# Edge sum of a graph kernel: block numbers loaded one word at a time, inside a step instead of ahead of it

## The chip, the cores and the metric

The kernel runs on one core of a Trainium2 chip. The metric is device time in microseconds, from one launch. Three runs of the kernel before gave 3587.72, 3590.77 and 3591.53 us; the median, 3590.77 us, is the time to compare with.

## What is computed

A graph has 12500 nodes with 64 features and 400000 edges, sorted by their target node `dst`. Three message-passing rounds run over the same edges: a mean over neighbours, then two convolutions that also add a projection of each edge's own 64 attributes. Since the projection is linear, the kernel needs the sum of the edge attributes at each target node only once; that sum is what the changed loop computes. Cut down to it:

```python
agg = segment_sum(x[src], dst);  deg = segment_sum(1, dst)
h = relu(concat(x, agg / max(deg, 1)) @ W_fc + b_fc) + x @ W_res + b_res
x1 = layernorm(x + h)
# each of the two convolutions:
msg = h[src] @ Wm + bm + edge_attr @ We + be     # segment_sum(edge_attr, dst) is shared by both
out = segment_sum(msg, dst) + h @ Ws + bs
# result: layernorm(x1 + conv2(relu(conv1(x1))))
```

## The kernel before

The 12500 nodes lie in 98 blocks of 128. The program has a preparation, then round 0, then the **edge sum**, then rounds 1 and 2. Each engine has its own instruction stream, written out by hand; semaphores order them. Only the edge sum is touched by the change. It starts about 1537 us into the profiled execution and ends at about 2021 us.

The 400000 edges are 625 groups of 5 x 128. The edge sum goes through `ESTEPS` = 728 steps; a step takes one group and the block of 128 target nodes to which it adds (a group that spans two blocks takes two steps). Which group and block a step has depends on the data, so both lists are made at the start of the program and kept on partition 0: group numbers as words in `path`, block numbers as bytes in `steps`, four to a 32-bit word. All buffers are rings of `EB` = 8, so step n uses slot h = n % 8. In one step:

- SyncE loads the group's edge attributes into `feats[h]` (L1540).
- GpSimd (POOL) makes `rel_e[h]`, the target's lane within the block for every edge (L1291), after VectorE has used the slot (`e_mark`).
- VectorE (DVE) compares `rel_e[h]` with the lane numbers and gets 0/1 marks, 128 x 640 in f16 (L921, the **comparison**). It waits for `e_hot` (ScalarE has read that slot's last marks; on even h, L919) and `e_rel` (L920).
- ScalarE (ACT) copies the marks of two steps to f32 (L1416), after `e_mark`, and signals `e_hot`.
- TensorE (PE) multiplies attributes by marks into PSUM bank h, 10 matmuls (L1179), and signals `e_mm[h]`.
- VectorE adds the PSUM bank of the step `LAG` = 6 before into the sum of its block, 128 x 128 in f32 (L932, the **addition**). It waits for `e_mm` (L929) and for its own last addition, `e_add` (L930), since two additions may go to the same block. The block is known only at run time: register operations, recorded at L932, cut the byte out of a loaded word and turn it into an address.

So VectorE's stream is comparison, addition, comparison, addition, with register operations between. The loop body is written out for `TURNS` = 7 rounds of the ring, 56 steps; the loop over it (L913) runs 13 times. The bytes come into registers by `load_blocks(frm, n)`: one load instruction (TENSOR_LOAD, at L466) that fetches n/4 words into n/4 registers of VectorE's sequencer. The returned list has four expressions for each word (a mask, or a shift and a mask); the trace shows them at L932, where they are used. Other places call it too: the sum of gathered rows in all rounds loads 8 bytes, two words, at a time. A similar helper `load` (L458) fetches words of `path`; VectorE calls it for one word at the end of each round.

Of the kernel before, what the change touches and what calls it, by code (L numbers as in the profile page):

```python
# [105 lines left out]
def gnn_program(nc, step_c, first_row, x, src, dst, edge_attr, W_fc, b_fc, W_res, b_res,  # L106
# [8 lines left out]
    D0, D1 = B0 * P, END * P  # L115
    REG, (RUNS, CSTEPS) = regions(), runs()
    BACK = max(k for _, _, _, k, _ in RUNS)
    CG = -(-CSTEPS // P)
    HIS = BLOCKS
# [13 lines left out]
    EB = 8  # L133
# [3 lines left out]
    TURNS = 7  # L137
# [10 lines left out]
    CH = 512 // VC  # L148
    CW = CG * P
    spans_of = [(s0, (REG + [(0, 0, 0, 0, CW)])[n + 1][4], wd) for n, (_, _, wd, _, s0) in enumerate(REG)]  # L150
    PIECES = 16
    HB, RING = 4, 16
# [13 lines left out]
    assert TP > WHOLE and WHOLE % 16 == 0 and BLOCKS <= P  # L166
    assert UNION >= YW >= BLOCKS * D and G * F1 <= 512 and 0 < GI <= ITERS and all(b <= 2 * GI or b - n >= 2 * GI for n, b in ((r[1], r[0] + r[1]) for r in REG)) and B0 >= 0 and DB % 2 == 0 and WPB % HB == 0
    assert all(n % 2 == 0 and s0 % P == 0 and sum(d) * WD // wd % RING == 0 for _, n, wd, ds, s0 in REG for d in ds) and HIS % 2 == 0 and (SETS - SETS % 2) * G >= T + BLOCKS - 1

    ctx = ExitStack()  # L170
    with ctx:
# [127 lines left out]
        sums_e = af[:, :].rearrange("p (b c) -> p b c", c=P)  # L299
# [163 lines left out]
        def load_blocks(frm, n):  # L463

            words = steps[0:1, :].bitcast(I32)
            _, packed = nc.values_load_multi_w_load_instructions(  # L466
                words[0:1, bass.ds(frm, n // 4)], engines=(ENG.DVE,), min_val=0,
                max_val=(BLOCKS - 1) * 0x01010101,
                skip_runtime_bounds_check_because="four block numbers, each clamped when the path was made")
            return [nc.s_assert_within(b, 0, BLOCKS - 1, skip_runtime_bounds_check_because="one of the four block numbers")  # L470
                    for v in packed for b in (v & 0x7F, (v >> 8) & 0x7F, (v >> 16) & 0x7F, v >> 24)]

        def flat(v):
            return v.rearrange("p b d -> p (b d)")
# [3 lines left out]
        def _(dve):  # L478
# [58 lines left out]
            for b in range(-(-CG // CH)):  # L537
                cols = slice(b * CH, min(b * CH + CH, CG))
                n = cols.stop - cols.start
# [90 lines left out]
            for b in range(3):  # L630
                cols = slice(b * GP, min(b * GP + GP, SG))
                n = cols.stop - cols.start
# [66 lines left out]
            for c0, c1, landed in ((0, SG // 2, s_g[0]), (SG // 2, SG, s_last)):  # L699
                dve.wait_ge(landed, 16 * (c1 - c0))  # L700
                n, cols = c1 - c0, slice(c0 * P, c1 * P)
# [25 lines left out]
            for r in range(3):  # L727
# [82 lines left out]
                if r == 0:  # L810
# [5 lines left out]
                    for b0, blocks, wd, deeps, s0 in REG:  # L816
                        upto, pair = steps_upto(wd, deeps)
                        many = at_once(wd)
                        with dve.Fori(0, blocks // 2) as i:
                            for j in range(2):  # L820
# [3 lines left out]
                                for q in range(upto[j][0], upto[j][WPB]):  # L824
                                    n, s = q % RING, bass.ds(i * pair + (q + s0), many)
# [11 lines left out]
                                    if part == 0:  # L837
                                        dve.wait_ge(b_used[j], it + (1 + j))
                                        if b0 < 2 * GI:
                                            bs = load_blocks((it * 2 + j) * (GW // 4), GW)  # L840
# [4 lines left out]
                                    elif part == 1:  # L845
                                        dve.wait_ge(b_red[j], it + 2)
                                        to = flat(acc_all[:, bass.ds(i * 2 + (b0 + B0 + j), 1), :])
                                        V.tensor_tensor(to, to, part_d[:, j, :], ALU.add).then_inc(s_add[0], 1)
                                    else:
                                        k = part - 2  # L850
                                        dve.wait_ge(s_add[0], before + (k + 1))
                                        if k < G:
                                            to = flat(acc[:, bass.ds(bs[k], 1), :])
# [7 lines left out]
                    for j in range(2):  # L861
# [4 lines left out]
                        to = acc[:, END - 2 + j, :]  # L866
# [5 lines left out]
                if r:  # L872
                    for first, end in ((0, GI), (GI, ITERS))[0:1 + (GI < ITERS)]:
                        with dve.Fori(0, end - first) as i:
                            for j in range(2):
# [8 lines left out]
                                to = feat[:, bass.ds(i * 2 + (first * 2 + B0 + j), 1), :]  # L884
# [27 lines left out]
                first_block = SETS * GW + GW + EDGE0 - LAG  # L912
                with dve.Fori(0, ESTEPS // EB, TURNS) as turn:  # L913
                    for n in range(EB * TURNS):
                        i, h = turn + n // EB, n % EB
                        if n % (2 * EB) == 0:
                            bs = load_blocks(turn * (EB // 4) + (first_block + n) // 4, min(2 * EB, EB * TURNS - n))
                        if h % 2 == 0:
                            dve.wait_ge(e_hot[h // 2], i + 1)  # L919
                        dve.wait_ge(e_rel[h], i + 1)  # L920
                        marks = V.tensor_tensor(mark_e[:, h, :, :].rearrange("p j (c u) -> p j c u", u=2),  # L921
                                                lane16[:, 0:P].rearrange("p (c u) -> p c u", u=2).unsqueeze(1)
                                                .to_broadcast([P, EG, P // 2, 2]),
                                                rel_e[:, h, :, :].unsqueeze(2).to_broadcast([P, EG, P // 2, 2]),
                                                ALU.is_equal)
                        if h % 2:
                            marks.then_inc(e_mark[h // 2], 1)
                        b = (h - LAG) % EB
                        dve.wait_ge(e_mm[b], i + (2 if h >= LAG else 1))  # L929
                        dve.wait_ge(e_add, i * EB + (h + EB))  # L930
                        to = flat(sums_e[:, bass.ds(bs[n % (2 * EB)], 1), :])
                        V.tensor_tensor(to, to, ps[:, b, 0:P], ALU.add).then_inc(e_add, 1)  # L932
                last = load_blocks((SETS * GW + ESTEPS + GW + EDGE0 - LAG) // 4, EB)
                for k in range(LAG):
                    dve.wait_ge(e_mm[EB - LAG + k], ESTEPS // EB + 1)
                    dve.wait_ge(e_add, ESTEPS + k + EB)
                    to = flat(sums_e[:, bass.ds(last[k], 1), :])
# [650 lines left out]
```

## Time and profile before

| | before |
|---|---|
| median of three runs | 3590.77 us |
| profiled execution: span | 3585.2 us |
| edge sum: stretch of the span | 1537 to 2021 us, 484 us |
| busy in that stretch: PE / DVE / ACT / POOL | 441.9 / 441.8 / 431.9 / 207.7 us |
| VectorE's comparison / addition, mean of one | 484 / 280 ns |
| loads at L466 in that stretch | 52: shortest 520 ns, median 965, longest 985 |
| mean transfer rate in that stretch | 246 GB/s |

The span runs from the first to the last instruction of the profiled execution. The single runs are 2.5 to 6.3 us above it; what the profile adds or leaves out at the ends is not in the table. PE, DVE, ACT, POOL and SP are TensorE, VectorE, ScalarE, GpSimd and SyncE. A "q" behind an engine's name marks an instruction that its sequencer runs itself (register arithmetic, loads into registers, branches): these are not counted as busy, and the engine proper may work meanwhile. A comparison and an addition in a row overlap by about 0.08 us at each seam, so busy time of a group can add up to more than the time that passes.

### The profile page before, as it was taken

What the parts mean: (1) busy time and instruction counts of PE and PEld (TensorE: products, weight loads), DVE (VectorE), ACT (ScalarE), POOL (GpSimd) and SP (SyncE); (2) the same over time, 40 slices, a digit from 0 to 9 for tenths busy, and PEclk for the clock granted to TensorE, in tenths of its full rate; (3) what the DMA queues carried; (4) which work ended last, traced back from release to release, by engine and by line L of the source; (5) the groups of instructions that cost most, each with busy time, mean ns of one, the idle gap of its engine ahead of it and who ended that gap; (6) DMA issues with size and microseconds to landing.
All of it is one profiled execution on the core that took longest, in us unless ns stands there. A gap on an engine that the chain in (4) does not pass through costs nothing.

```text
span 3585.2 us, 114923 instructions
## 1 busy us (share of the span) xinstructions
PE 3167.6 (88%) x39408; PEld 2958.1 (83%) x39408; DVE 2339.3 (65%) x5369; ACT 1613.7 (45%) x2096; POOL 2021.8 (56%) x2292
## 2 busy tenths in 40 slices
PE   0239999999999999889999889999999889999995
PEld 0127988888888888778888879999999889999995
DVE  8779998888888888779999682333333423333335
ACT  0123677878999999788988650000000400000000
POOL 6761234445666666534444256666666666666664
PEclk9869999999999999999999979999999999999998
DMA  3521455556666666668888429999999599999996
GB/s 92 134 18 70 167 194 198 218 213 233 238 240 251 251 238 240 245 207 247 248 246 247 147 93 400 403 402 402 402 402 403 202 354 403 402 402 402 402 402 241
DMA packets 232872, 959.10 MB, mean 268 GB/s; under 512 B 44815, under 2 KB 144285, under 8 KB 173818
## 3 DMA queue, kind: packets, MB, share of 16 engines
q1 hardware_dynamic: 186027, 884.48, 65.0%
q0 software_dynamic: 46784, 73.84, 6.8%
q8 instruction: 33, 0.54, 0.1%
q14 instruction: 28, 0.23, 0.0%
HBM read 694.75 MB, written 263.40 MB: 267 GB/s over the span
## 4 chain that ended last, share of the span: by engine, by line
PE 68%; DVE 11%; issue 8%; POOL 6%; DVEq 3%; ACT 2%; DMA 2%; SPq 0%; ACTq 0%; POOLq 0%
PE ps L1109 48%; PE ps L1132 10%; DVE union L805 5%; PE ps L1179 4%; PE ps L1101 3%; POOL abuf L1213 3%; DVE union L921 2%; ACT union L1416 1%; DVE abuf L932 1%; POOL union L1213 1%; PE ps L1069 1%; DVEq L466 1%; DVEq L932 1%; PE ps L1188 1%; POOL abuf L1255 0%
## 5 line engine op out<-in xcount | busy, mean ns | idle before, releaser
L1271 POOL DMA_INDIRECT msg<-y_tab,idx x1368 | 1531.1, 1119 | 1041.9 <-ACT idx L1377 652.0
L1109 PE MATMUL ps<-union,abuf 128*128 128x192 bf16 x14896 | 1265.3, 247 | 13.9 <-DVEq L782 10.2
L1109 PEld LDWEIGHTS ps<-union,abuf 128*128 128x128 f16 x14896 | 1226.7, 98 | 21.2 <-issue 10.6
L1398 ACT ACTIVATE abuf<-ps 128x784 f16<-128x784 f32 x1216 | 1000.7, 823 | 239.9 <-PE ps L1132 212.3
L805 DVE TENSOR_TENSOR union<-lane,union 128x1568 f16<-128x1568 f16 (+3 forms) x1440 | 949.5, 710 | 31.0 <-PE ps L1132 27.1
L1109 PE MATMUL ps<-early,abuf 128*128 128x195 bf16 x7546 | 853.4, 249 | 0.0
L1109 PEld LDWEIGHTS ps<-early,abuf 128*128 128x128 f16 x7546 | 677.1, 99 | 100.9
L1132 PE MATMUL ps<-union 128*128 128x392 f16 (+2 forms) x4288 | 689.5, 288 | 52.4 <-DVE union L805 47.1
L1377 ACT ACTIVATE idx<-src_g 128x6 int32 (+1 forms) x228 | 46.4, 205 | 1280.2 <-PE ps L1101 1277.9
L1179 PE MATMUL ps<-union 128*64 128x128 f32 x7280 | 444.4, 278 | 48.2 <-ACT union L1416 48.1
L1179 PEld LDWEIGHTS ps<-union 128*64 128x64 f32 x7280 | 394.1, 137 | 98.4 <-DVE abuf L932 79.2
L1416 ACT ACTIVATE union<-union 128x1280 f32<-128x1280 f16 x364 | 432.9, 1259 | 55.9 <-DVE union L921 53.9
L797 DVE TENSOR_TENSOR acc<-acc,ps 128x64 f32 (+1 forms) x918 | 203.7, 222 | 364.2 <-DVE acc L797 211.2
L1132 PEld LDWEIGHTS ps<-union 128*128 128x128 f16 x4288 | 362.9, 108 | 92.3 <-issue 48.3
L921 DVE TENSOR_TENSOR union<-lane,rel_e 128x640 f16<-128x640 f16 x728 | 352.5, 484 | 41.7 <-issue 40.3
L1291 POOL TENSOR_TENSOR rel_e<-early,base_e 128x10 f16 x728 | 208.4, 305 | 287.5 <-DVE union L921 271.1
L880 DVE TENSOR_REDUCE part_d<-ps 128x64 f32<-128x192 f32 x152 | 54.4, 358 | 459.2 <-PE ps L1109 459.2
L786 DVE TENSOR_TENSOR hot_g<-code_g,lane 128x768 f16<-128x768 f16 x228 | 218.0, 956 | 70.2 <-DVE acc L797 69.2
L932 DVE TENSOR_TENSOR abuf<-abuf,ps 128x128 f32 x728 | 203.5, 280 | 1.8 <-PE ps L1179 1.1
L1101 PE MATMUL ps<-msg,hot_g 128*128 128x64 bf16 (+1 forms) x4104 | 167.2, 194 | 5.5 <-DMA msg<-y_tab,idx 5.5
L1101 PEld LDWEIGHTS ps<-msg,hot_g 128*128 128x128 f16 x4104 | 157.0, 98 | 6.0 <-DMA msg<-y_tab,idx 6.0
L854 DVE TENSOR_TENSOR acc<-acc,ps 128x65 f32 x456 | 99.5, 218 | 56.8 <-DVE acc L854 37.9
(229 smaller groups left out, 1241.4 us busy)
## 6 DMA issues: line engine op xcount, KB each, us to landing
abuf<-a_dram SPq DMA_DIRECT2D x304, 1568.0 KB
a_dram<-abuf SPq DMA_DIRECT2D x76, 3136.0 KB
union<-in_edge_attr_dram SPq DMA_DIRECT2D x728, 160.0 KB, 2.9
msg<-y_tab,idx POOLq DMA_INDIRECT x1368
y_tab<-union SPq DMA_DIRECT2D x28, 336.0 KB, 2.2
abuf<-in_x_dram SPq DMA_DIRECT2D x28, 224.0 KB, 3.4
y_tab<-early SPq DMA_DIRECT2D x7, 682.5 KB, 5.5
out_dram<-union SPq DMA_DIRECT2D x2, 800.0 KB, 3.5
```

The lines of the kernel that those rows point to most:

```text
L786: V.tensor_tensor(hot_g[:, j * G:(j + 1) * G, :], code_g[:, bass.ds((it * 2 + j) * G, G)].unsqueeze(2).to_broadcast([P, G, P]), lane16[:, ...
L805: return V.tensor_tensor(to.rearrange("p s (c u) -> p s c u", u=2), lanes.unsqueeze(1).to_broadcast([P, n, width // 2, 2]), codes[:, which ...
L921: marks = V.tensor_tensor(mark_e[:, h, :, :].rearrange("p j (c u) -> p j c u", u=2), lane16[:, 0:P].rearrange("p (c u) -> p c u", u=2).uns ...
L932: V.tensor_tensor(to, to, ps[:, b, 0:P], ALU.add).then_inc(e_add, 1)
L1101: last = nc.tensor.matmul(tile_ps(r, j, k), hot_g[:, s, :], msg[:, s, c * width_of[r]:(c + 1) * width_of[r]], start=c == 0, stop=c == 2)
L1109: last = nc.tensor.matmul(ps[:, bank, 0:3 * width_of[r]], abuf[:, buffer, hi * P:(hi + 1) * P], ycols[r][:, hi, :], start=hi == 0, stop=hi ...
L1132: nc.tensor.matmul(ps[:, w % 4, 0:WIN].rearrange("p (h d) -> p h d", d=WD)[:, :, d0:d0 + wd], hot_c[:, n, WIN:WIN + P], hot_c[:, n, 0:HIS ...
L1179: last = nc.tensor.matmul(ps[half:half + D, h, 0:P], feats[:, h, j * D:(j + 1) * D], hot_e[:, h, j, :], start=j < 2, stop=j >= EG - 2)
L1271: pool.indirect_dma_start(msg[:, s, 0:3 * width_of[r]], None, y_tab[r], bass.IndirectOffsetOnAxis(ap=idx[:, s:s + 1], axis=0)).then_inc(ga ...
L1291: nc.gpsimd.tensor_tensor(rel_e[:, h, :, :], flat(dst_e[:, bass.ds(grp[h], 1), :]).unsqueeze(2) .to_broadcast([P, EG, 2]), base_e[:, bass. ...
L1398: A.activation(abuf[:, j, :].rearrange("p (h w d) -> p w h d", w=WPB, d=WD) [:, w:w + 2, :, :], ps[:, w % 4:w % 4 + 2, 0:WIN].rearrange("p ...
L1416: A.activation(hot_e[:, h:h + 2, :, :], mark_e[:, h:h + 2, :, :], ACT.Copy)\
```

## The change

Before, VectorE loads block numbers ahead of the comparison of every sixteenth step of the body: at n = 0, 16 and 32 four words, at n = 48 the two words that are left. Afterwards it loads one word at every fourth step, and the load stands between the comparison and the addition of that step. In the 56 steps of a body that is 14 loads of one word in place of 4 loads with 14 words together; over the 13 passes, 182 loads in place of 52. The same bytes reach the same additions. Nothing else differs.

```diff
                 with dve.Fori(0, ESTEPS // EB, TURNS) as turn:
                     for n in range(EB * TURNS):
                         i, h = turn + n // EB, n % EB
-                        if n % (2 * EB) == 0:
-                            bs = load_blocks(turn * (EB // 4) + (first_block + n) // 4, min(2 * EB, EB * TURNS - n))
                         if h % 2 == 0:
                             dve.wait_ge(e_hot[h // 2], i + 1)
                         dve.wait_ge(e_rel[h], i + 1)
@@ -925,10 +923,12 @@
                                                 ALU.is_equal)
                         if h % 2:
                             marks.then_inc(e_mark[h // 2], 1)
+                        if n % 4 == 0:
+                            bs = load_blocks(turn * (EB // 4) + (first_block + n) // 4, 4)
                         b = (h - LAG) % EB
                         dve.wait_ge(e_mm[b], i + (2 if h >= LAG else 1))
                         dve.wait_ge(e_add, i * EB + (h + EB))
-                        to = flat(sums_e[:, bass.ds(bs[n % (2 * EB)], 1), :])
+                        to = flat(sums_e[:, bass.ds(bs[n % 4], 1), :])
                         V.tensor_tensor(to, to, ps[:, b, 0:P], ALU.add).then_inc(e_add, 1)
```

## Rows read from the trace of the kernel before

**Rows 1.** Edge sum, busy us: PE, PEld, DVE, ACT, POOL; PEclk, DMA share, GB/s.

```profile
1537.00:2021.00 484.00, 441.88 (x7240) 391.97 (x7240) 441.79 (x1456) 431.94 (x364) 207.73 (x725) 0.99 0.81 246
```

**Rows 2.** Waits in the edge sum: us in total, times, longest us.

```profile
ACT union L1416 <- DVE union L921: 53.9, 55, 4.8
...
DVE union L921 <- issue: 40.3, 51, 1.3
DVE union L921 <- POOL rel_e L1291: 1.4, 1, 1.4
DVE abuf L932 <- PE ps L1179: 1.1, 2, 0.6
```

**Rows 3.** VectorE in order of time, around a four-word load inside the body.

```profile
1882.96 0.28 DVE L932 TENSOR_TENSOR abuf<-abuf,ps 128x128 f32 x1
1884.03 0.49 DVE L921 TENSOR_TENSOR union<-lane,rel_e 128x640 f16<-128x640 f16 x1 [0.79 <-issue]
1884.43 0.28 DVE L932 TENSOR_TENSOR abuf<-abuf,ps 128x128 f32 x1
```

**Rows 4.** The chain, 1902.6 to 1906.9 us: start us, us, what.

```profile
1903.82 0.06 DVEq L466
1903.87 0.04 issue
1903.91 0.29 DVEq L466
...
1904.48 0.02 DVEq L920
...
1904.55 0.09 DVE union L921
...
1904.69 0.04 DVEq L932
1904.73 0.03 issue
1904.77 0.06 DVEq L932
...
1906.69 0.07 issue
1906.76 0.06 DVE abuf L932
```

**Rows 5.** VectorE in order of time, around the two-word load and the loop's end.

```profile
1903.92 0.28 DVE L932 TENSOR_TENSOR abuf<-abuf,ps 128x128 f32 x1
...
1904.95 0.28 DVE L932 TENSOR_TENSOR abuf<-abuf,ps 128x128 f32 x1
...
1909.15 0.28 DVE L932 TENSOR_TENSOR abuf<-abuf,ps 128x128 f32 x1
...
1911.09 0.28 DVE L932 TENSOR_TENSOR abuf<-abuf,ps 128x128 f32 x1
```

**Rows 6.** The chain across the loop's end, 1909 to 1911.8 us.

```profile
1909.53 0.97 DVEq L466
1910.50 0.03 issue
...
1910.68 0.09 DVE union L921
```

**Rows 7.** Loads at L466 in the edge sum: ns min/median/max.

```profile
L466 DVEq TENSOR_LOAD <-steps x52: 520/965/985, 1548.3 to 2020.6; - x52
```

**Rows 8.** VectorE's loads of one word at L458, whole span.

```profile
L458 DVEq TENSOR_LOAD <-path x3: 321/322/323, 1513.7 to 3553.0; - x3
```

**Rows 9.** A two-word load in round 0, then VectorE's work in that window.

```profile
L466 DVEq TENSOR_LOAD <-steps x1: 525/525/525, 844.4 to 844.4; - x1
...
843.82 1.64 DVE L805 TENSOR_TENSOR union<-lane,union 128x512 f16<-128x512 f16 x3
```

**Rows 10.** ScalarE's copies in the edge sum, in order of time.

```profile
1899.26 6.07 ACT L1416 ACTIVATE union<-union 128x1280 f32<-128x1280 f16 x5
```

## The prediction

> **What bounds the kernel now.** I read first how busy each engine is in the edge sum, since nothing else is touched. In its 484 us TensorE and VectorE are both busy for 442 us and ScalarE for 432 us [rows 1]. Three engines near 90% say only that none has much room, so the next view is who waits for whom. ScalarE idles 53.9 us in 55 waits, all for VectorE's comparison, and VectorE idles 40.3 us in 51 waits that the trace calls "issue": no semaphore is late, its own sequencer has not delivered the next instruction. VectorE waits 1.4 us for GpSimd and 1.1 us for TensorE in the whole stage [rows 2]. So VectorE sets the pace, the others follow, and the only idle time of VectorE is made in its sequencer. There were 52 loads in the stage [rows 7] and 51 such waits.
>
> The timeline gives the pace. From the addition at 1904.95 to that at 1909.15 there are 7 steps, 4.20 us, so 0.60 us a step without a load [rows 5]. 728 steps of 0.60 are 436.8 us. ScalarE's five copies in 6.07 us, the last of them about 1.26 us long, are 1.20 us for two steps [rows 10]: that is VectorE's pace handed on, and its 364 copies could run in 437 us at most.
>
> **What the old loads cost.** Addition to addition across a load, less 0.60:
> - four words inside the body: 1884.43 - 1882.96 = 1.47, an excess of 0.87 us [rows 3]; two in each pass (n = 16 and 32);
> - two words at n = 48: 1904.95 - 1903.92 = 1.03, an excess of 0.43 us [rows 5];
> - four words at the loop's end, with the branch: 1911.09 - 1909.15 = 1.94, an excess of 1.34 us [rows 5].
>
> One pass: 2 x 0.87 + 0.43 + 1.34 = 3.51 us. Thirteen passes: 45.6 us. Check: 436.8 + 45.6 = 482.4 of 484 us [rows 1]. This is the whole amount that the change can move; it vanishes and is replaced by what the new loads cost.
>
> **What one new load takes.** The trace has four words at 0.965 us (median) and two at 0.52 [rows 7, 9], and three loads of one word on the same engine at 0.321 to 0.323 us [rows 8]. The line through the longer ones (0.22 us a word) gives 0.30. I take 0.32, the measured one. Those three ran while VectorE was idle, the new ones run under a comparison. The nearest row for that: in round 0 a two-word load that began at 844.4 and took 0.525 lies wholly inside three f16 comparisons in a row that kept VectorE busy from 843.82 to 845.46 [rows 9]; it took no longer than others, nor did the sequencer wait for the engine to drain. So bounds are 0.30 below and 0.525 (a two-word load) above, and the value lies near the lower one.
>
> The Trainium skill, "DMA: Bandwidth & Descriptors", section "Latency and other measured facts", speaks against this change: it gives a floor of about 600 ns for a `tensor_load` and says that the compiler unrolls it four times to amortize that. By it, the 182 new loads would cost 0.28 us more each than I reckon, an estimate of +51 us on the sum below, and the kernel would end near 3630 us. The trace disagrees already: a two-word load takes 0.52 us and a one-word load 0.32 [rows 7, 8].
>
> **How much of it is covered.** Before, the load ended and only then could the comparison be sent. Now the comparison is sent first and the load runs beside it; but the addition's address needs the word, so all that follows the load in the sequencer stands in front of the addition. Step by step, for a body load:
> - The sequencer ends its wait for `e_rel` (L920) 0.07 us before the previous addition starts (1906.69 against 1906.76) [rows 4].
> - From that wait's end to the first register operation of L932, without a load between, 0.19 us (1904.50 to 1904.69): the comparison is sent and the value for L930 is made [rows 4].
> - Into this comes an address operation of 0.06 us and 0.04 behind it [rows 4], the load of 0.32 [rows 8], and 0.03 behind the load [rows 6]: 0.45 us.
> - L932's register operations: 1904.69 to 1904.83, 0.14 us; and 0.05 from a sequencer's instruction to the start on an idle engine (L920's end 1904.50, comparison 1904.55) [rows 4].
>
> That is 0.83 us from L920, so 0.76 from the previous addition, against 0.60. With the rows' rounding 0.14 to 0.17; I take 0.15 us. The comparison covers the other 0.3 us of every load. The wait for the addition before (`e_add`) is over by then and costs nothing more. There are 13 such loads in a pass.
>
> At the loop's end the old load of 0.97 and 0.03 behind it go, so the comparison starts at 1910.68 - 1.00 = 1909.68 [rows 6]. Then 0.14 to L932's operations, 0.35 for the load (no address operation stood at this place), 0.14 and 0.05: the addition at 1910.36, 1.21 after the one at 1909.15, an excess of 0.61 us.
>
> One pass: 13 x 0.15 + 0.61 = 2.56 us; thirteen passes: 33.3 us. Saved: 45.6 - 33.3 = 12.3 us. The profiled execution would have a span of 3585.2 - 12.3 = 3572.9 us, and the median, 5.6 us above its span, becomes 3590.8 - 12.3 = **3578.5 us**, 0.34% less. The lever is long: 10 ns on each of 182 loads are 1.8 us.
>
> **What is queued behind the load.** On VectorE the waits for `e_mm` and `e_add`, the addition, and then the next comparison. A late addition keeps only VectorE waiting: TensorE may overwrite a bank after an addition made two steps earlier, which always comes before the comparison that TensorE needs anyway. The late next comparison reaches ScalarE, TensorE and GpSimd, as the old stalls did, now in portions of 0.15 and 0.61 instead of 0.43 to 1.34 us. With the stage at about 471 us, ScalarE (437) and TensorE (442 busy) stay under it. DMA share is 0.81 of its engines at 246 GB/s [rows 1] and would be asked for 3% more. Rounds 1 and 2 start earlier and stay as they are.
>
> **Rivals.**
> - *The one-word load costs what a two-word load costs, 0.525 us* (slower). It would be a price of each load rather than of each word, or a load stretched under an f16 comparison. 0.205 x 182 = 37.3 us more: 3616 us. From 0.39 us a load on (12.3 / 182 = 0.07 above 0.32) the kernel is slower. Against it are rows 8 and 9. Chance 0.12.
> - *More register work in front of the addition* than before: another address operation per load, or one that used to lie in the comparison's shade. One of 0.10 us (0.06 and its gap [rows 4]) on every load: +18.2, 3597 us; on half of them no change in the time. The trace cannot show how the new address is made. Chance 0.15.
> - *More cover*: the sequencer runs ahead of the engine. If it reaches the load some 0.10 us sooner than by L920's row, the excess is 0.05: 13 x 13 x 0.10 = 16.9 us less, 3562 us. For it: the engine finishes the addition before the comparison starts, while the sequencer has sent both. Against: the order of L920, comparison, L930 in the chain leaves it no such lead. Chance 0.12.
> - *The gain goes elsewhere*: stalls spread evenly leave ScalarE or GpSimd no pause to catch up, and VectorE begins to wait for `e_rel` or `e_mm`. In stretches of 16 steps at 0.60 us it waited for neither [rows 2], and the new mean step of 0.65 is slower than that. Time near 3590. Chance 0.06.
>
> **How the numbers follow.** The forecast has a chance of 0.50; its own range is 3572 to 3585 us (load of 0.29 to 0.36 us). Another 0.05 is for what I do not see. A measurement of this kernel can tell about 0.2%, 7.2 us, from no change. Faster than 3583.6: most of the forecast (0.46), the case of more cover (0.12) and a little of the rest (0.02), 0.60. Within: 0.20, from the forecast's edge, half or more of the register case and the last rival. Slower than 3598: 0.20, from the dear load, the rest of the register case and the unseen. For 8 in 10 the range must take in most of the cover case and most of the register case but not the dear load: 3563 to 3600 us.
>
> **What would show it.** In the profile after: 182 loads at L466's successor in the stage, of 0.30 to 0.33 us; VectorE's "issue" waits moved from the comparison to the addition at n % 4 = 0; additions 0.75 us apart there and 0.60 elsewhere; at the loop's end 1.21 instead of 1.94; the stage 471 to 472 us. ScalarE's waits for the comparison fall from 53.9 to about 42 us. The prediction is wrong if loads are longer than 0.39 us, if more than one register operation stands around each load, or if VectorE's waits name GpSimd or TensorE.

## The result

The changed kernel is slower: 3654.68 us (median of five runs, 3644.68 to 3668.36) against 3588.83 (five runs, 3585.16 to 3591.53). The ratio is 1.0185, with a 95% interval of 1.0162 to 1.0208. I had forecast 3578.5 us, 0.34% faster, with a range of 3563 to 3600.

In the three later sets of runs the kernel before fell into two groups, near 3588 and near 3608 us (14 of 25, 10 of 23 and 10 of 32 runs in the upper one), and so did some variants; the groups are treated below, and the length of the edge sum does not depend on them.

The waits of the changed kernel in the edge sum, total us, times, longest; they answer to [rows 2]:

```profile
engine line waited for: us in total, times, longest us
...
ACT union L1416 <- DVE union L919: 94.2, 134, 5.2
...
DVE union L919 <- issue: 45.2, 12, 4.6
DVE abuf L932 <- issue: 15.2, 60, 0.3
...
DVE abuf L932 <- PE ps L1179: 11.6, 26, 0.6
```

VectorE's "issue" waits ahead of the comparison (L919 now) were 51 of 40.3 us together. There are 12 left, and they last 45.2 us: one for each return of the loop, up to 4.6 us. The waits of the addition are new. The 60 "issue" waits of 15.2 us look like those that I had foreseen at the loads, but they are not: by their place in the pass, 13 stand at its first step and 39 at the short pauses at steps 14, 34 and 54 that are described below, and only 8 elsewhere; at a load in the body the engine idles only 0.03 to 0.06 us, 0.10 at most. And there are 26 waits for TensorE, 11.6 us against 1.1. The loads themselves are not to blame, as the source view of L466 in the stage shows (ns min/median/max):

```profile
L466 DVEq TENSOR_LOAD <-steps x183: 299/305/541, 1537.1 to 2078.1; - x183
```

Around one load in the body, in order of time, and the chain there, which answers to [rows 4]:

```profile
1904.40 0.28 DVE L932 TENSOR_TENSOR abuf<-abuf,ps 128x128 f32 x1
1904.60 0.48 DVE L919 TENSOR_TENSOR union<-lane,rel_e 128x640 f16<-128x640 f16 x1
1905.13 0.29 DVE L932 TENSOR_TENSOR abuf<-abuf,ps 128x128 f32 x1
```

```profile
1904.50 0.30 DVEq L466
...
1904.95 0.04 DVEq L932
1905.00 0.03 issue
1905.03 0.06 DVEq L932
1905.09 0.05 issue
1905.13 0.12 DVE abuf L932
```

Addition to addition is 0.73 us: an excess of 0.13. So far the forecast holds. Then the loop's end, which answers to [rows 6]:

```profile
1909.70 0.04 DVEq L913
1909.74 0.03 issue
1909.77 0.06 DVEq L913
1909.83 0.25 DVE abuf L932
1910.08 4.42 issue
1914.50 0.05 DVEq L913
...
1914.67 0.10 DVE union L919
```

The closing branch runs at 1909.77, and the next instruction of the loop (L913) starts at 1914.50. Between them VectorE's sequencer does nothing and waits for nothing that has a semaphore. This return is the longest of the twelve: from the start of the branch to that of the next instruction they take 3.4 to 4.7 us, 3.9 in the mean. In the kernel before, the same two instructions lay 0.3 us apart, and the load followed:

```profile
1909.12 0.06 DVEq L913
1909.18 0.25 DVE abuf L932
1909.43 0.06 DVEq L913
1909.49 0.04 issue
1909.53 0.97 DVEq L466
```

A pause of this kind in each pass is new, and the page of the profile says what happens in it. The queue lists, before and after (packets, MB, share of 16 engines):

```profile
q14 instruction: 28, 0.23, 0.0%
```

```profile
q14 instruction: 88, 0.72, 0.1%
```

60 more packets of instructions, five for each of the 12 returns of the loop, of 8192 bytes each; if the short pauses described below, 128 instructions apart, lie at their bounds, that is 64 bytes an instruction. VectorE's loop is fetched anew in every pass, as the later runs bear out. The program has 115183 profiled instructions against 114923: 260 more, 20 for each of 13 passes (14 loads and 13 address operations where there were 4 and 3). The loop has 360 instructions instead of 340.

The pause has a sequel on TensorE. Busy us by stretch (PE, PEld, DVE, ACT, POOL, then the granted clock, DMA share and GB/s), for most of a pass, the pause, what follows it, and the pass after:

```profile
1880.00:1910.00 30.00, 29.26 (x470) 25.28 (x468) 28.63 (x92) 27.85 (x24) 13.63 (x44) 1.00 0.84 246
1910.00:1914.60 4.60, 2.52 (x41) 2.04 (x40) 0.08 (x1) 1.19 (x1) 0.36 (x2) 1.00 0.85 251
1914.60:1924.00 9.40, 6.29 (x62) 6.29 (x64) 7.12 (x22) 6.21 (x5) 2.85 (x10) 0.64 0.29 84
1924.00:1953.00 29.00, 28.25 (x457) 24.30 (x453) 27.73 (x89) 26.80 (x22) 13.63 (x44) 1.00 0.83 246
```

TensorE stood still for 5 us (to 1917.7), and for a good part of the next 9 us its granted clock was at the lower of its two levels, 1.2 instead of 2.4 GHz. The products of the first steps came late, and VectorE's additions waited for them:

```profile
1919.63 0.29 DVE L932 TENSOR_TENSOR abuf<-abuf,ps 128x128 f32 x1 [0.36 <-PE ps L1179]
...
1921.71 0.29 DVE L932 TENSOR_TENSOR abuf<-abuf,ps 128x128 f32 x1 [0.61 <-PE ps L1179]
```

The lower clock came back where it costs more. After the edge sum TensorE folds the sums (L1188), which took some 22 us at full clock before. Before, and then after (same columns):

```profile
2025.00:2045.00 20.00, 19.72 (x177) 19.72 (x177) 1.24 (x3) 5.97 (x10) 0.00 (x0) 1.00 0.00 1
```

```profile
2082.00:2102.00 20.00, 19.63 (x100) 19.64 (x100) 1.30 (x3) 3.45 (x6) 0.00 (x0) 0.55 0.00 1
2102.00:2122.00 20.00, 20.00 (x96) 20.00 (x95) 0.00 (x0) 3.12 (x6) 0.00 (x0) 0.50 0.00 0
```

196 folding products took 22.1 us before and 40.4 after. No pause of the loop stands right ahead of them: the clock was full from 2046.6 to 2084.2 us (PEclk is 1.00 from 2047 to 2082), and TensorE had idled 1.4 us between its last edge product and the first folding product. Whether the pauses have a part in this fall is not shown; the runs e5 and e11 below are about it. In sum, of the two profiled executions (3664.1 against 3585.2 us, 78.9 more): 57.1 in the edge sum, 20.4 between its last addition and round 1's first dense product (145.8 against 125.4), 1.4 in the rest. The profiled execution is one of the two slowest of the five. The two fastest, 3644.68 and 3650.21 us, lie 56 and 61 us above the median of before, which is about what the edge sum alone takes, and their mean clock is higher (0.959 against 0.954 and 0.955); so the 20 us of the folding probably belong to some of the runs only.

### The profile page after: what moved, and what is told of

It is laid out like the page before. It is cut to its first block, busy times and chain, and to the rows that moved or that the text cites. A ratio compares the mean times of both kernels' runs of the same rounds, so it can differ in the third digit from the quotient of the medians.

```text
span 3664.1 us, 115183 instructions
## 1 busy us (share of the span) xinstructions
PE 3222.9 (88%) x39408; PEld 3003.6 (82%) x39408; DVE 2358.7 (64%) x5369; ACT 1629.4 (44%) x2096; POOL 2030.2 (55%) x2292
## 4 chain that ended last, share of the span: by engine, by line
PE 65%; DVE 12%; issue 10%; POOL 6%; DVEq 4%; DMA 2%; ACT 1%; SPq 0%; POOLq 0%; ACTq 0%
PE ps L1109 47%; PE ps L1132 10%; DVE union L805 5%; PE ps L1101 3%; POOL abuf L1213 3%; DVE union L919 3%; DVE abuf L932 2%; PE ps L1179 2%; DVEq L466 1%; DVEq L932 1%; PE ps L1188 1%; POOL union L1213 1%; PE ps L1069 1%; DMA abuf<-in_x_dram 1%; ACT union L1416 0%
## 5 line engine op out<-in xcount | busy, mean ns | idle before, releaser
L1179 PE MATMUL ps<-union 128*64 128x128 f32 x7280 | 478.6, 286 | 70.9 <-ACT union L1416 61.2
L1179 PEld LDWEIGHTS ps<-union 128*64 128x64 f32 x7280 | 418.2, 143 | 131.3 <-DVE abuf L932 110.1
L1416 ACT ACTIVATE union<-union 128x1280 f32<-128x1280 f16 x364 | 448.6, 1268 | 97.3 <-DVE union L919 94.2
L1291 POOL TENSOR_TENSOR rel_e<-early,base_e 128x10 f16 x728 | 220.0, 321 | 332.9 <-DVE union L919 316.8
L919 DVE TENSOR_TENSOR union<-lane,rel_e 128x640 f16<-128x640 f16 x728 | 352.8, 485 | 46.6 <-issue 45.2
L932 DVE TENSOR_TENSOR abuf<-abuf,ps 128x128 f32 x728 | 206.2, 283 | 35.1 <-issue 15.2
```

The source lines that it names most:

```text
L1179: last = nc.tensor.matmul(ps[half:half + D, h, 0:P], feats[:, h, j * D:(j + 1) * D], hot_e[:, h, j, :], start=j < 2, stop=j >= EG - 2)
L1291: nc.gpsimd.tensor_tensor(rel_e[:, h, :, :], flat(dst_e[:, bass.ds(grp[h], 1), :]).unsqueeze(2) .to_broadcast([P, EG, 2]), base_e[:, bass. ...
L1416: A.activation(hot_e[:, h:h + 2, :, :], mark_e[:, h:h + 2, :, :], ACT.Copy)\
```

## The experiments

The columns of the table below are read from each profile: the mean time from one closing branch of the loop to the next; the edge sum from the first comparison to the last; and q14's packets. "Place" is where the loop's last instruction falls if VectorE's stream is counted in blocks of 128 from the block in which the loop begins: three blocks end at 384. It comes from the trace of the changed kernel. Beside the pause at the loop's end it shows three shorter ones of about 0.33 us in a pass, ahead of the 96th, the 224th and the 352nd instruction, 128 apart; the loop therefore begins at the 34th instruction of a block. (The addition of the last step is sent before the branch and starts after it; it is not counted to the next pass. When the expectations below were written I had counted it, and their places are one too low.) Kernel before: 33 + 340 = 373. After: 33 + 360 = 393, nine over.

| run | place of the loop's end | pass, us | edge sum, us | q14 | median, us (runs) |
|---|---|---|---|---|---|
| before | 373 | 37.15 | 483.6 | 28 | 3588.8 (5) |
| after | 393 | 41.89 | 540.7 | 88 | 3654.7 (5) |
| e1 after, shifted 104 | 369 | 36.02 | 469.5 | 29 | 3582.7 (10) |
| e2 before, shifted 19 | 392 | 44.07 | 567.1 | 88 | 3687.2 (4) |
| e3 before, shifted 104 | 349 | 37.20 | 483.9 | 29 | 3599.1 (10) |
| e4 two words, late | 379 | 36.59 | 476.6 | 28 | 3582.9 (10) |
| e5 after, shifted 97 | 362 | 35.97 | 469.4 | 30 | 3595.4 (12) |
| e6 before, shifted 12 | 385 | 44.32 | 569.3 | 89 | 3695.1 (2) |
| e7 before, shifted 13 | 386 | 44.33 | 569.6 | 88 | 3694.2 (2) |
| e8 before, 60 products | 373 | 37.13 | 483.4 | 28 | 3600.3 (12) |
| e9 one word, early, shifted 97 | 362 | 37.14 | 482.8 | 29 | 3607.7 (8) |
| e10 four words, late | 373 | 36.85 | 479.9 | 28 | 3585.8 (8) |
| e11 before, 8 products | 373 | 37.15 | 483.5 | 28 | 3588.2 (12) |
| e12 after, shifted 98, 8 products | 363 | 36.03 | 469.6 | 30 | 3573.6 (9) |

n increments moved the loop by n - 1 instructions: so many more instructions of VectorE stand ahead of it in the traces, and the short pauses of e2, e6 and e7 lie where they should by it (ahead of the 77th, the 84th and the 83rd instruction). The 98 inside a branch are taken as 98; no trace shows them, since they do not run. Each set of runs has its own runs of the kernel before, on the same chip: median 3605.0 of 25 beside e1 to e4, 3592.2 of 23 beside e5 to e8 (on another chip than e1 to e4 and e9 to e12), 3590.6 of 32 beside e9 to e12.

**Is it the code's position?** The loop is left alone and moved.

```diff
                 step(V.memset(sums_e[:, 0:HALF, :], 0.0))
+                for _ in range(105):              # e1 on the changed kernel, e3 on the one before; e2: 20
+                    dve.sem_inc(s_pad, 1)
                 dve.wait_ge(s_lde, 32)
```

> The changed kernel, with 105 idle semaphore increments on VectorE ahead of the edge sum, which move its loop 104 instructions further into VectorE's instruction stream. Theory A (code reloads: the loop of 360 instructions lies over four blocks of 128 instructions and is fetched again in every pass; moved, it lies within three): VectorE's queue of instruction fetches falls from 88 packets to about 30, the 4.3 us pause at each loop end falls to about 0.7, the stage is 470 us, and the time is 3575 to 3582 us (some us of the increments themselves included). Rival B (the loads themselves or their place are dear, whatever the code's position): no change, about 3655 us.

Measured: 3582.66 us, ratio to before 0.9953 (0.9932 to 0.9973). The page's line for the fetch queue:

```profile
q14 instruction: 29, 0.24, 0.0%
```

The pauses are gone, with every load still there. The edge sum is 14.1 us shorter than before. The time is at the upper end of the forecast plus 0.7 us, because the increments took 0.093 us each, 9.7 us together.

> The kernel before, untouched in its loop, with 20 idle increments ahead of it: the loop of 340 instructions moves 19 further and now ends 7 instructions inside a fourth block. Theory A: it gets the pauses of the changed kernel: about 58 us more in the edge sum and 20 us more behind it, since TensorE's clock is at its lower level there: 3650 to 3670 us. Rival B: 3589 to 3590 us, as before.

Measured: 3687.15 us, ratio 1.0228 (1.0177 to 1.0279). The old loop, untouched, gets the pauses, and they cost more than I expected: 83 us more in the edge sum, not 58. The chain at a return of its loop:

```profile
1928.07 4.22 issue
1932.29 0.09 DVEq L916
1932.38 0.04 issue
1932.41 0.96 DVEq L467
```

A pause of 4.22 us, and behind it still the four-word load of 0.96: the two add up. (Lines are shifted by the increments' three.)

> The kernel before with 105 idle increments, five times as many as in the run with 20; its loop lies within three blocks again. Theory A: 3589 to 3594 us, the increments' own time alone. If idle increments themselves cost time (rival C): more than the run with 20.

Measured: 3599.13 us, ratio 1.0007 (0.9982 to 1.0031); 7 of 10 runs lie at 3595.9 to 3600.8, some 10 us above the lower group of before, which is what 105 increments take. Rival C is out: more increments cost less than 20 did. These three runs show the cause: the loop's position in VectorE's stream, not what is in it.

**Is there an edge?** The increments stand further down from here on, where VectorE waits for the target rows.

```diff
+                for _ in range(13):               # e6 on the kernel before; e7: 14; e5, on the changed one: 98
+                    dve.sem_inc(s_pad, 1)
                 dve.wait_ge(s_pc, 1 + 2 * BC + BE)
```

> The kernel before with 13 idle increments. Its loop moves by 12 instructions, and by the positions read from the trace of the changed kernel its last instruction, the closing branch, is the last of the third block. Theory A, if a loop may fill three blocks to the last instruction: passes of 37.1 us, 28 or 29 fetches, 484 us for the edge sum. If the fetch looks ahead of the branch: already slow, passes of 41 us or more.

> One increment more than in the run with 13: the closing branch is the first instruction of a fourth block. Theory A: 88 fetches, a pause of about 4 us in every pass, passes of 41 to 42 us, an edge sum of 540 us and more. A cause that grows with the number of instructions (and has no edge) would show no difference between 13 and 14.

Measured: both slow and alike, 3695.13 and 3694.23 us, passes of 44.3 us, 89 and 88 fetches. For e6 I had written down a look ahead of the branch as the alternative, but the trace shows that the place was off by one instead. One of e6's short pauses stands in every pass right ahead of the closing branch, which is therefore the first instruction of the fourth block and not the last of the third. The chain at a return of e6 (L916 is the loop's line: first its register operation, then the branch):

```profile
1842.13 0.04 DVEq L916
1842.17 0.07 issue
1842.24 0.27 DVE abuf L935
1842.51 0.04 issue
1842.55 0.06 DVEq L916
1842.61 4.49 issue
1847.11 0.09 DVEq L916
```

and the same two instructions in e2, where the border lies elsewhere:

```profile
1927.69 0.04 DVEq L916
1927.73 0.03 issue
1927.76 0.06 DVEq L916
```

The branch starts 0.42 us after the register operation in e6 and 0.07 in e2. In e7 the pause stands one instruction earlier, ahead of the register operation. So both runs are past the border, no look ahead is needed to explain them, and no run has a loop that ends exactly at it. There is an edge: the old loop is fast where it ends at 373 and slow from 385 on, 12 instructions of shift cost as much as 13, and 104 cost nothing; with e4, fast at 379, the first slow place lies between 380 and 385.

**What are the loads worth without the pause?**

> The changed kernel with 98 idle increments, now placed where VectorE waits some 7 us for the target rows to be prepared, so that they cost 1 to 2 us instead of 9.7. Theory A (code position): the loop lies in three blocks, the edge sum is 14 to 15 us shorter than in the kernel before, and the time is 12 to 14 us under the lower of the two groups into which the runs of the kernel before fall (3587 us), so 3573 to 3576 us. Rival: the gain of the run with 105 increments came from something else that the increments did; then this one is not faster by what the increments no longer cost.

Measured: 3595.41 us, ratio 0.9989 (0.9969 to 1.0009). The edge sum is as expected, 469.4 us, 14.2 less than before. The time is not: 11 of 12 runs lie at 3590.9 to 3599.1, one at 3580.5. The profile has the reason, in the folding behind the edge sum:

```profile
2015.00:2035.00 20.00, 19.89 (x104) 19.89 (x104) 1.07 (x3) 3.58 (x6) 0.00 (x0) 0.57 0.01 1
2035.00:2055.00 20.00, 19.95 (x94) 19.76 (x93) 0.00 (x0) 3.59 (x7) 0.00 (x0) 0.50 0.00 0
```

The clock was at the lower level from 2017.6 on and the folding took 39.9 us, with no pause in the loop at all: the pauses are not needed for this fall. TensorE had idled 1.5 us ahead of the folding. What this kernel won in the edge sum, it lost to the clock. The increments also delayed the loop by 4 us, not by 1 to 2.

> The changed kernel with two words at every eighth step instead of one at every fourth, at the same place in the step. Its loop has 346 instructions and, unshifted, ends 6 short of the fourth block. Theory A: no pauses; a two-word load in front of the addition costs 0.34 us (0.13 measured for one word, and 0.21 for the second), so 6 x 0.34 + 0.92 = 3.0 us a pass against 3.5 before: 3581 to 3584 us. Rival B (place of the load): clearly slower than before, half the loads, so some 30 us more.

```diff
-                        if n % 4 == 0:
-                            bs = load_blocks(turn * (EB // 4) + (first_block + n) // 4, 4)
+                        if n % 8 == 0:
+                            bs = load_blocks(turn * (EB // 4) + (first_block + n) // 4, 8)
...
-                        to = flat(sums_e[:, bass.ds(bs[n % 4], 1), :])
+                        to = flat(sums_e[:, bass.ds(bs[n % 8], 1), :])
```

Measured: 3582.92 us, ratio 0.9976 (0.9949 to 1.0003), 7 of 10 runs at 3580.1 to 3584.9. The excess is 0.35 us for a body load and 0.82 at the loop's end, 2.9 us a pass (3.0 reckoned); the edge sum is 7.0 us shorter. No pause, and nothing is shifted: 346 instructions fit where 360 do not.

> One word at every fourth step, but ahead of the comparison as in the kernel before, with 98 covered increments so that the loop lies in three blocks. It differs from the covered shifted run of the changed kernel in the place of the load alone. Theory (the load's place is worth the difference between a stall of 0.22 us ahead of the comparison, by the old stalls' slope of 0.22 us a word, and 0.13 us behind it): 13 x 0.22 + 0.68 = 3.5 us a pass over 33.6, so passes of 37.1 us against 35.97, and an edge sum of 484 us against 469.4. If the place is worth nothing: 36.0 us a pass.

```diff
+                        if n % 4 == 0:
+                            bs = load_blocks(turn * (EB // 4) + (first_block + n) // 4, 4)
                         if h % 2 == 0:
                             dve.wait_ge(e_hot[h // 2], i + 1)
...
-                        if n % 4 == 0:
-                            bs = load_blocks(turn * (EB // 4) + (first_block + n) // 4, 4)
```

Measured: passes of 37.14 us and 0.22 us of excess for a body load, as expected; 3607.69 us, ratio 1.0017 (0.9992 to 1.0042).

> The old four loads, moved between comparison and addition: the place alone. By the sum, 0.79 us for four words and 0.35 for two in the body, 1.33 at the loop's end: 3.26 us a pass, passes of 36.9 us, an edge sum of 480 us, 3 to 4 us less than before; 28 fetches, no pauses.

Measured: passes of 36.85 us, 0.79 us for four words and 0.35 for two in the body, 1.26 at the loop's end; 3585.76 us, ratio 0.9969 (0.9945 to 0.9994). The two runs part the two halves of the change. Splitting the loads, but leaving them ahead of the comparison, gives nothing (37.14 against 37.15). Moving them alone gives 0.30 us a pass. Both together give 1.18 (e5: 35.97): behind a comparison, a load of one, two or four words costs 0.08 to 0.09 us less than ahead of it (0.13 against 0.22, 0.35 against 0.43, 0.79 against 0.88), and fourteen short loads gain that fourteen times, 1.2 us.

**What are the two groups of times?**

```diff
+                    pe.wait_ge(e_add, ESTEPS + LAG + 1)
+                    for k in range(60):           # e8; e11 and e12: 8
+                        nc.tensor.matmul(ps[0:D, 0, 0:P], feats[:, 0, 0:D], hot_e[:, 0, 0, :], start=True, stop=True)
                     pe.wait_ge(e_add, ESTEPS + LAG + EB)
```

> The kernel before with 60 extra matrix products on TensorE between its last edge step and the folding that follows, written to a bank that the folding overwrites; they fill about 3.6 us in which TensorE waits for VectorE's last additions. Theory: the 20 us by which runs of one and the same kernel differ (3587 and 3608 us) are TensorE's clock at its lower level during the folding; with the products TensorE does not pause and all runs lie in the lower group, 3587 to 3592 us. Rival: the clock falls whatever TensorE does there, and the two groups stay.

Measured: 3600.31 us, 12 runs at 3597.7 to 3603.1, one group only; beside it 10 of 23 runs of before lie at 3604.8 or above. I had mis-sized the products: 13.3 us, not 3.6, so the gain is paid for and the ratio is 1.0006 (0.9988 to 1.0024).

> The kernel before with 8 extra matrix products (about 1.8 us) instead of 60 between the last edge step and the folding. Theory: TensorE's idle time there, 1.8 us in the profiled run, is what lets its clock fall in part of the runs; with it filled, all runs lie near 3588 us. If the 60 products held the clock up by the time that they took and not by filling the gap, the two groups come back.

Measured: 3588.21 us, 12 runs at 3584.5 to 3591.9; of 32 runs of before beside it, 10 lie above 3606. Ratio 0.9986 (0.9971 to 1.0002). TensorE's timeline:

```profile
2021.13 4.90 PE L1179 MATMUL ps<-union 128*64 128x128 f32 x80 [0.33 <-ACT union L1419]
2025.86 1.91 PE L1185 MATMUL ps<-union 128*64 128x128 f32 x16
2027.76 4.46 PE L1191 MATMUL ps<-twofold,abuf 128*128 128x64 f32 x38
```

1.9 us of work in place of 1.8 us of idling, and the upper group does not appear. At the share of before, 22 of 32 in the lower group, twelve of twelve would come by chance once in 90 times; with e8 and e12 it is 33 of 33. The groups themselves show in the clock: the mean granted clock of the runs of before is 0.965 to 0.967 in the lower group and 0.960 to 0.962 in the upper one, and 20 us more at half clock in 3600 would be 0.0055. Not every kernel without the products has an upper group either (e1 and e10 have none in 10 and 8 runs, e5 has 11 of 12 in it), so the products remove it, but its share without them is not explained.

**The version that the runs point to.** The changed kernel, shifted, with the eight products; the increments stand in a branch that these inputs do not take, so they fill room and cost no time.

```diff
                 with dve.If(more > 0):
+                    for _ in range(0 if r else 98):
+                        dve.sem_inc(s_pad, 1)
                     with dve.Fori(0, more) as i:
```

> The changed kernel, moved into three blocks by 98 increments that stand in a branch which is not taken with these inputs (they take room and no time), and with the 8 products ahead of the folding. Theory: 14 us less in the edge sum, no increments to pay for, clock kept up in the folding: 3573 to 3577 us in all runs, against 3588 and 3608 of the kernel before. If skipping the increments costs a fetch of its own, some 2 to 4 us more.

Measured: 3573.63 us, 9 runs at 3570.8 to 3577.3, ratio to before 0.9941 (0.9920 to 0.9962). Faster than either kernel: 15 us under the lower group of before, 35 under the upper. Its edge sum (columns as above):

```profile
1537.00:2016.00 479.00, 462.49 (x7327) 400.72 (x7328) 457.74 (x1464) 444.04 (x365) 226.11 (x728) 0.99 0.83 249
```

It is the change as forecast, with the code in the right place and the products added. Against e11, the kernel before with the same products on the same chip (3588.21), it is 14.6 us less, which is the 13.9 us of the edge sum (469.6 against 483.5) and little else. The increments are a crutch, since their number is right for this program alone.

## Why the prediction was wrong

- *VectorE sets the pace and its only idle time is in its sequencer*: right; in the slow kernel too it is the sequencer that is idle.
- *The old loads cost 3.51 us a pass*: right; with the mean of all passes it is 3.55, and what e5 saves (14.2 us) fits it.
- *A one-word load takes 0.32 us, under a comparison too*: right, 0.305 in the median of 183. The rule of the Trainium skill, "DMA: Bandwidth & Descriptors", section "Latency and other measured facts", that I had weighed (a floor of some 600 ns) does not hold here.
- *0.15 us of excess for a body load*: 0.12 to 0.13 measured. *0.61 at the loop's end*: 0.62 in e5. *The edge sum saves 12.3 us*: 14.2 in e5. *The comparison covers the other 0.3 us*: right in amount, but little of that comes from the new place; ahead of the comparison the same load costs 0.22 (e9), so the place gives 0.09.
- **The step that failed**: "At the loop's end the old load of 0.97 and 0.03 behind it go ... an excess of 0.61 us." In the changed kernel that excess is 4.2 us in the mean of the twelve returns. I counted the added instructions only by their own time and cost their room in the stream at nothing. None of my rivals had it. "More register work in front of the addition" counted the same instructions and again only their durations.
- The size of the miss, from the trace: a pass of the changed kernel takes 41.89 us against 35.97 in e5, 5.9 more. 3.6 are the pause at the return, 1.0 the three short ones at block borders, and the other 1.3 fall in steps 6 to 12 of a pass, where the additions wait for a TensorE at the lower clock. Twelve returns: 71 us. Against them stand the 14 us that the new loads do save, so 57 in the edge sum. The folding at the lower clock adds 20 in the profiled execution; e5 shows the same fall without any pause, so those 20 are not shown to come from the change.
- *What is queued behind the load; the others stay under VectorE*: right for the loads, but the chain pause, clock, late products was not thought of, nor the folding behind the stage. The sign of being wrong that I had named, waits of VectorE for TensorE, did come, 11.6 us of them. "Rounds 1 and 2 start earlier and stay as they are" was wrong in its first half.

Was it to be foreseen? The trace of before held a hint: 28 packets of instructions in the page, and in the stage only three of them, all in the loop's first pass; so a loop of 340 instructions was not fetched again over 12 returns, and how near it was to the limit could have been asked. The place within its block, on which all hangs, I found only from the pauses of the changed kernel.

The Trainium skill, "Runtime: NRT & Kernel Launch", section "Instruction fetch mechanics", describes a mechanism of this kind: an engine other than TensorE keeps two blocks of 16 KiB (512 instructions together), and a taken branch whose target is not in them waits for a fetch. The trace agrees as far as it goes: a loop of 360 instructions, well under 512, is fetched again in every pass when it lies badly, and a return then costs some 4 us. Here the packets have 8 KiB and the short pauses are 128 instructions apart. Whether what must be met is "within three blocks of 128" or "within two of 256, fetched in halves" stays open: every variant run here fits both or neither.

Also open: whether a loop that ends exactly at the border is still fast, and why the clock falls ahead of the folding in some runs and not in others of one and the same program. In all 33 runs in which TensorE's gap ahead of the folding was filled the mean clock is that of the lower group of times, 0.965 or more, so the gap bears on it; what decides in the others is not shown. Passes of the shifted old kernel (e2, 44.1 us) are 2.2 us longer than those of the changed one (41.9): 1.0 of it lies at the loop's end, where the load behind the pause is 0.66 us longer, 0.8 in the body's loads, and 0.7 in steps 6 to 12, less 0.3 for the short pauses; why its pauses and late products last longer is open.

## What to carry to other kernels

A loop body written out for many steps has a size and a place, and both can decide: count its instructions, see in the page how many packets the instruction queue moves, and if it is near a limit, ask what an added instruction does at the closing branch before asking what it does in its step. A stall of some us on one engine costs more than its length when TensorE starves behind it, because the clock comes back late; a gap of under 2 us ahead of a long run of products may be worth filling with idle ones. A sum that holds to 20 ns for each load (0.13 against 0.15 here) says nothing of costs that are not in any instruction.

## What the runs showed of the hardware that I had not expected

- Reloading a loop: 3.4 to 4.9 us from the start of the closing branch to the next instruction (medians 3.8 in the changed kernel, 4.3 in e2, e6 and e7; 0.3 without), and pauses of 0.33 us within the pass, 128 instructions apart; twelve to thirteen instructions of shift turn a kernel of 3589 us (lower group) into one of 3694 to 3695 us.
- Idle semaphore increments cost VectorE's sequencer 0.093 us each.
- Loads into VectorE's registers under a comparison take 0.305 us for one word, 0.524 for two (e4) and 0.963 for four (e10); ahead of it four words took 0.965, and one word while VectorE was idle 0.32 [rows 8].
- Granted clock during the folding: 1.00 for the whole of it (22 us) or 0.50 for nearly all of it (40 us), after a gap of under 2 us in TensorE's work (1.7 us in the profile of before, 1.5 in that of e5); one and the same program has runs 20 us apart, with mean clocks that differ by the same amount.
